# A four-layer graph network: more gathers in flight, source tables split from on-chip memory, and a new order of the steps in layer 1's edge stage

## The chip, the cores and the metric

One core of one Trainium2 chip runs the whole kernel. The time is the device time of one execution in microseconds. Matrix products run on TensorE (PE), element-wise work on VectorE (DVE) and ScalarE (ACT), indirect DMAs are issued by GpSimd (POOL), most plain DMAs by SyncE (SP).

## What is computed

Node features x (6250 nodes, 64 wide) go through four graph layers; each ends in a residual addition and a layer norm. There are 206250 edges (src, dst), sorted by dst, with 64 features each. Layer 0 is a hypergraph convolution, layer 1 an edge network, layer 2 a gated convolution, layer 3 a LightGCN sum. The change touches layers 1 and 2:

```python
# layer 1, H = 128
edge_in = concatenate([edges, nodes[receivers], nodes[senders]])
h = relu(edge_in @ We1 + be1)
agg = segment_sum(h @ We2 + be2, receivers)
# layer 2
gate = sigmoid(k[dst] + q[src])
agg = segment_sum(gate * v[src], dst)
```

For layer 1 the two node products are made once per node: one table for target rows (tab[4]) and one for source rows (tab_src[4]), both 128 wide. An edge then adds its target row, its source row and its own features times a 64x128 weight, takes the relu and is summed at its target node.

## The kernel before, in words

**Windows and chunks.** The nodes stand in NB = 49 blocks of 128. Each block of target nodes has a window of 36 tiles of 128 edges. In layer 1, 25 of the windows (the slots kind) hold their edges sorted by source block into 49 groups of 128 slots, so that the source rows as well as the target rows can be picked by PE with 0/1 selection matrices. The other 24 (the natural kind) keep their edges in their own order; there only the target row is picked by PE, and the source rows are fetched from tab_src in HBM by POOL, with one indirect DMA (gather) per tile of 128 edges. A slots window is worked off in 7 chunks of 7 blocks, a natural one in 6 chunks of 6 tiles. One window of each kind makes a pair: 13 steps, alternating slots, natural, ..., slots, numbered q = 0 to 12. There are 24 pairs, and a last slots window with 7 steps. Twenty-four natural windows of 36 tiles make 864 gathers.

**Tables in three parts.** For exact products every f32 table is split into three bf16 parts: ACT copies to bf16 (first part), DVE subtracts (rest), ACT copies again (second part), DVE subtracts (third part); L1693, L2251, L1697 and L2255, in seven pieces each. Before a layer's edge stage two tables are split: the target table (dtab into dsplit) and the source table (qtab into qsplit). Both are first stored from the arena (NW, NV) to HBM (L767 to L771) and loaded again by SP (L645, L647), because the target table needs another node order. NW and NV hold the linear layer's results; NV is copied out of PSUM by ACT. Layer 2 uses the same routine with a target table 64 wide. In layer 1 POOL gathers need the stored source table; in layer 2 nothing does but the load.

**The order of a step in layer 1's edge stage (edge_pairs, one function on each engine).** Each engine has its own queue, in program order, and waits on semaphores. In step q, before the change:
- SP (load_pair, L676 to L691) loads the selection rows and features of the chunk; rings of four slots and three natural buffers.
- PE (body, L1386): transposes the features of chunk q (transpose_features, L1325), makes the pre-activation of chunk q-2 by selecting rows and multiplying features (meet: L1348 source rows, L1353 target rows, L1359 features), and sums the messages of chunk q-4 at their targets (add_up, L1379).
- ACT (body, L1757): copies the transposed features out of PSUM (keep_features, L1734; two fT buffers, so that it waits for PE's meet of q-2), stores the selection matrices of slots chunks for layer 2 (store_hots), and takes the relu of chunk q-2 (messages: L1744 slots, L1747 natural). A natural relu waits for DVE's addition of the gathered rows, a slots relu for PE's meet and for the sum of the chunk before last, whose hid buffer it takes.
- DVE (body, L2421): for a natural chunk adds the gathered rows to the pre-activation of q-2 (add_sources, L2381), makes the row selection of q (L2347), then the residual (second part) of the messages of q-2 (L2394), the sum selection of q (L2330 slots, L2364 natural) and the last part of q-2 (L2401). PE's add_up waits for the last part.
- POOL (gather_sources, L943) issues the gathers (L967) into a ring of three qgot buffers. Before each it waits until the one four tiles earlier has landed (LIVE = 4 semaphores feat_put), and before a chunk that reuses a buffer for DVE's addition. At the start of each pair it loads the pair's source row numbers (gidx, L953) and waits for them.

Before this, POOL's queue holds the feature puts (put_features, L920), 900 indirect DMAs that place the edge features into the slots layout; they began in the stage before layer 0.

```python
def earlier(j, odd, q, back):
    return (j, odd, q - back) if q >= back else (j - 1, 1 - odd, SEQ + q - back)
...
    act.wait_ge(fT_made, count_at(j, q))
    if not isinstance(j, int) or j > 0 or q >= 2:
        act.wait_ge(pre_made, count_at(j, q) - 2)
```

Of the kernel before, what the change touches and what calls it, by code (L numbers as in the profile page):

```python
# [19 lines left out]
E = 206250  # L20
D = 64
H = 128
# [43 lines left out]
def build(nc, x, src, dst, feat, W1, b1, W2, b2, We1, be1, We2, be2, Wn1, bn1, Wn2, bn2,  # L66
# [11 lines left out]
    with ctx:  # L78
# [46 lines left out]
        NV = carve(76, NB * H).rearrange("p (b f) -> p b f", b=NB)  # L125
# [126 lines left out]
        dtab = carve(73.5, NB * H)  # L252
        qtab = carve(98, NB * H)
# [118 lines left out]
        tabs_in = [sem(f"tabs_in{i}") for i in range(2)]  # L372
# [35 lines left out]
        gate_out = sem("gate_out")  # L408

# [26 lines left out]
        TAB_STORES = [16, 32, 48, 64, 32, 64, 80]  # L436
# [103 lines left out]
        def gathers_landed(eng, j, tiles):  # L540

            for i in range(LIVE):
                if tiles > i:
                    eng.wait_ge(feat_put[i], j * (PUTS * 16) + (NS * PUTS * 16 + (tiles - i + LIVE - 1) // LIVE * 16))

        @block.sync
        def _(sp):
# [93 lines left out]
            def slots(k):  # L641
# [4 lines left out]
                    .then_inc(tabs_in[0], 16)  # L646
                sp.dma_start(qtab, nodes(tab_src[k])).then_inc(tabs_in[1], 16)  # L647
# [87 lines left out]
            def general(k):  # L735
                w = W_TAB[k]
                sp.wait_ge(tab_stored_g if k < 4 else tab_stored, TAB_STORES[k])

# [24 lines left out]
            for k in range(4, 7):  # L763
                w = W_TAB[k]
                sp.wait_ge(tab_ready, k + 1)
                if k == 4:
                    sp.dma_start(nodes(tab[4]), NW[:, :, :].rearrange("p b f -> p (b f)")).then_inc(tab_stored, 16)  # L767
                    sp.dma_start(nodes(tab_src[4]), NV[:, :, :].rearrange("p b f -> p (b f)")).then_inc(tab_stored, 16)
                elif k == 5:
                    sp.dma_start(tab[5].rearrange("(p b) f -> p b f", p=P), NW[:, :, 0:D]).then_inc(tab_stored, 16)  # L770
                    sp.dma_start(nodes(tab_src[5]), NV[:, :, :].rearrange("p b f -> p (b f)")).then_inc(tab_stored, 16)  # L771
                else:
                    sp.dma_start(tab[k].rearrange("(p b) f -> p b f", p=P), NW[:, :, 0:D]).then_inc(tab_stored, 16)
# [16 lines left out]
        def _(pool):  # L790
# [21 lines left out]
            def general(k):  # L812
                w = W_TAB[k]
                pool.wait_ge(tab_stored_g if k < 4 else tab_stored, TAB_STORES[k])
                idx = lambda c: bass.IndirectOffsetOnAxis(ap=gcol[:, c:c + 1].bitcast(u32), axis=0)
# [127 lines left out]
            def gather_sources():  # L943

                pool.wait_ge(tab_stored, TAB_STORES[4])
                pool.wait_ge(splits_lo, 2 * NC)

                def body(j, odd, first=False):
                    start = pool.value_load(start_i[0:1, bass.ds(j + NS, 1)], min_val=0, max_val=E - WE)
                    if not isinstance(j, int) or j >= 2:  # L950
                        for i in range(LIVE):
                            pool.wait_ge(feat_put[i], j * (PUTS * 16) + (NS - 1) * (PUTS * 16))
                    pool.dma_start(gidx[odd][:, :], src[bass.ds(start, WE)].rearrange("(p t) -> p t", p=P)).then_inc(gidx_in, 16)  # L953
                    for n in range(NCH):
# [7 lines left out]
                        for t in range(TN):  # L962
                            tile = n * TN + t
                            i = tile % LIVE
                            pool.wait_ge(feat_put[i], j * (PUTS * 16) + (NS * PUTS * 16 + tile // LIVE * 16))
                            pool.nop(nofuse=True)
                            pool.indirect_dma_start(qgot[n % 3][:, slot_of[t] * P:(slot_of[t] + 1) * P], None, tab_src[4],  # L967
                                                    bass.IndirectOffsetOnAxis(ap=gidx[odd][:, tile:tile + 1].bitcast(u32), axis=0))\
                                .then_inc(feat_put[i], 16)
                body(0, 0, first=True)  # L970
                body(1, 1)
                with pool.Fori(1, PAIRS_N // 2) as i:
                    body(i * 2, 0)
                    body(i * 2 + 1, 1)

# [11 lines left out]
        def _(pe):  # L987
# [321 lines left out]
            def edge_pairs():  # L1309
# [182 lines left out]
        def _(act):  # L1492
# [190 lines left out]
            def slots(k):  # L1683
# [42 lines left out]
            def edge_pairs():  # L1726
# [9 lines left out]
                def messages(j, odd, q):  # L1736

                    kind, c = place(j, q)
                    i = (q + odd) % 2
                    if kind == "slots":  # L1740
# [64 lines left out]
        def _(dve):  # L1805
# [434 lines left out]
            def slots(k):  # L2240
# [4 lines left out]
                for i, (tb, sp_, wd) in enumerate(((dtab, dsplit, w_), (qtab, qsplit, H))):  # L2245
                    t3 = tb[:, 0:NB * wd].rearrange("p (b f) -> p b f", b=NB)
                    s3 = sp_[:, 0:NB * 3 * wd].rearrange("p (b s f) -> p b s f", b=NB, s=3)
                    with dve.Fori(0, NC) as c:
                        at = bass.ds(c * CH, CH)
                        dve.wait_ge(splits_hi, c + (1 + NC * (2 * m + i)))  # L2250
                        V.tensor_tensor(t3[:, at, :], t3[:, at, :], s3[:, at, 0, :], ALU.subtract).then_inc(splits_res, 1)  # L2251
# [300 lines left out]
```

## Time and profile before

| | us |
|---|---|
| median of 3 runs | 4964.16 (4954.04 to 4967.15) |
| the profiled execution, its own time | 4958.28 |
| its span | 4956.7 |
| busy in the span: PE / PE weight load | 4118.4 (83%) / 3710.4 (75%) |
| busy: DVE / ACT / POOL | 3063.9 (62%) / 1450.4 (29%) / 2552.3 (51%) |
| mean granted TensorE clock | 0.92 |

The busy shares are means over stages with different limits, so a change in one stage is read from that stage's windows, waits and timelines. Idle time in brackets stands before the instruction it belongs to, with what ended it. x3 means three instructions merged into one row, with the time from the first one's start to the last one's end. Matmuls are pipelined, and the end that a row shows overlaps the next one's start by up to 0.16 us, so that steps are measured from start to start.

### The profile page before, as it was taken

The page shows a single profiled execution, that of the slowest core. Times are in us where ns is not written, and L with a number is a line of the kernel's source. Part 1 is how long each engine was busy: PE and PEld are TensorE (multiplying, and loading weights), DVE is VectorE, ACT ScalarE, POOL GpSimd, SP SyncE. Part 2 cuts the span into 40 slices and gives each one's busy share as a digit, 9 for nine tenths or more (in the row PEclk, how much of TensorE's full clock was granted, in tenths as well). Part 3 has the DMA queues.
Part 4 walks back from the last instruction along what each step waited for, and adds up shares of the span by engine and source line. Part 5 has one row for each costly group of instructions (what it writes and reads, how often), then busy time and mean ns, then how long its engine had stood idle before and what let it go on. Part 6 is the DMA issues. An engine that isn't in the chain of part 4 may idle for free.

```text
span 4956.7 us, 144137 instructions
## 1 busy us (share of the span) xinstructions
PE 4118.4 (83%) x56332; PEld 3710.4 (75%) x56332; DVE 3063.9 (62%) x4215; ACT 1450.4 (29%) x2353; POOL 2552.3 (51%) x2291
## 2 busy tenths in 40 slices
PE   1777799987999981999999999899758989999596
PEld 0566688887999981777777777777548988888596
DVE  5999888881111023777777777777437777777612
ACT  0333599990000012222222222222222222222100
POOL 0388766665665676666666666666003433333200
PEclk9766899998999995999999999999859999999798
DMA  5510488889999955776676777677326766666496
GB/s 173 203 30 29 144 317 321 323 320 315 397 383 417 417 199 187 226 232 220 227 235 228 227 235 229 224 230 236 128 78 219 235 207 205 221 221 214 135 399 260
DMA packets 430602, 1170.77 MB, mean 236 GB/s; under 512 B 111223, under 2 KB 250470, under 8 KB 422760
## 3 DMA queue, kind: packets, MB, share of 16 engines
q1 hardware_dynamic: 331910, 929.09, 53.0%
q0 software_dynamic: 66016, 114.12, 7.9%
q10 hardware_dynamic: 32256, 121.34, 6.2%
q8 instruction: 340, 5.57, 0.4%
q14 instruction: 80, 0.66, 0.0%
HBM read 798.21 MB, written 368.14 MB: 235 GB/s over the span
## 4 chain that ended last, share of the span: by engine, by line
DMA 41%; issue 27%; POOL 16%; PE 9%; DVE 4%; POOLq 2%; SPq 1%; ACT 0%; ACTq 0%; DVEq 0%
DMA feat_slot<-SK,sidx_p 18%; DMA arena<-tab_l_src,SK 17%; POOL arena L843 6%; POOL feat_slot L920 5%; POOL arena L967 4%; PE PS L1254 4%; DMA sidx_p<-SK 2%; DMA SK<-in_src_dram 2%; PE PS L1422 1%; PE PS L1023 1%; PE PS L1426 0%; SPq L460 0%; POOLq L890 0%; SPq L461 0%; PE PS L1442 0%
## 5 line engine op out<-in xcount | busy, mean ns | idle before, releaser
L920 POOL DMA_INDIRECT feat_slot<-SK,sidx_p x900 | 1114.1, 1238 | 568.7 <-DMA feat_slot<-SK,sidx_p 294.7
L967 POOL DMA_INDIRECT arena<-tab_l_src,SK x864 | 976.5, 1130 | 525.0 <-DMA arena<-tab_l_src,SK 241.8
L843 POOL TENSOR_TENSOR arena<-arena 128x448 f32<-128x448 f32 x343 | 365.6, 1066 | 808.6 <-DVE arena L2287 808.6
L1422 PE MATMUL PS<-arena 128*128 128x128 bf16 x7203 | 651.8, 221 | 124.5 <-DVE arena L2330 64.9
L1254 PE MATMUL PS<-arena 128*128 128x192 bf16 (+1 forms) x7203 | 615.4, 248 | 107.5 <-DVE arena L2130 61.9
L1254 PEld LDWEIGHTS PS<-arena 128*128 128x128 bf16 x7203 | 607.0, 98 | 114.4 <-DVE arena L2130 62.2
L1426 PE MATMUL PS<-arena 128*128 (+1 forms) x7203 | 610.4, 194 | 0.0
L1353 PE MATMUL PS<-arena 128*128 (+1 forms) x6267 | 591.4, 223 | 0.0
L1422 PEld LDWEIGHTS PS<-arena 128*128 128x128 bf16 x7203 | 457.4, 99 | 148.0 <-issue 138.0
L1426 PEld LDWEIGHTS PS<-arena 128*128 128x128 bf16 x7203 | 446.0, 99 | 1.1
L1353 PEld LDWEIGHTS PS<-arena 128*128 128x128 bf16 x6267 | 427.8, 100 | 3.8
L1379 PE MATMUL PS<-arena 128*128 128x384 bf16 x2089 | 414.9, 336 | 2.1 <-DVE arena L2401 2.1
L1348 PE MATMUL PS<-arena 128*128 128x128 bf16 x3675 | 408.1, 220 | 7.5 <-DVE arena L2330 7.5
L2394 DVE TENSOR_TENSOR arena<-arena 128x896 f32<-128x896 f32 (+1 forms) x319 | 328.4, 1029 | 125.0 <-ACT arena L1744 112.3
L1711 ACT ACTIVATE arena<-PS 128x448 f32<-128x448 f32 x343 | 186.8, 544 | 730.1 <-PE PS L1426 730.1
L1190 PE MATMUL PS<-arena 128*128 128x128 bf16 x4802 | 344.9, 220 | 39.8 <-DVE arena L2076 19.5
L1325 PE MATMUL PS<-ident,arena 128*128 128x128 f32 x1132 | 184.5, 281 | 228.4 <-ACT arena L1734 124.2
L2280 DVE TENSOR_TENSOR arena<-arena,PS 128x448 f32<-128x448 f32 x343 | 212.0, 618 | 240.1 <-ACT arena L1711 217.6
L2076 DVE TENSOR_TENSOR arena<-sd,iota 128x1792 bf16<-128x1792 bf16 x343 | 351.7, 1083 | 10.1 <-DMA nat_rows<-arena 10.1
L2381 DVE TENSOR_TENSOR arena<-PS,arena 128x768 f32<-128x768 f32 x144 | 137.8, 957 | 351.6 <-DMA arena<-tab_l_src,SK 308.4
L1325 PEld LDWEIGHTS PS<-ident,arena 128*128 128x128 f32 x1132 | 137.7, 142 | 289.3 <-issue 133.2
L1359 PE MATMUL PS<-wtwo,arena 64*128 64x128 f32 x4178 | 349.4, 294 | 0.0
(254 smaller groups left out, 6957.0 us busy)
## 6 DMA issues: line engine op xcount, KB each, us to landing
arena<-slot_rows SPq DMA_DIRECT2D x343, 448.0 KB
arena<-cnt_t SPq DMA_DIRECT2D x147, 896.0 KB
hots<-arena ACTq DMA_DIRECT2D x175, 672.0 KB
arena<-hots SPq DMA_DIRECT2D x175, 672.0 KB
arena<-cnt_t SPq DMA_DIRECT2D x147, 672.0 KB
cnt_t<-arena SPq DMA_DIRECT2D x49, 1568.0 KB
cnt_s<-arena SPq DMA_DIRECT2D x49, 1568.0 KB
arena<-cnt_s SPq DMA_DIRECT2D x49, 896.0 KB
```

Of the source, the lines that this page charges most:

```text
L843: pool.tensor_tensor(hid3[i][:, 2 * n:3 * n], hid3[i][:, n:2 * n], upper3[i][:, n:2 * n], ALU.subtract)\
L920: pool.indirect_dma_start(feat_slot, bass.IndirectOffsetOnAxis(ap=sidx_p[odd][:, n:n + 1].bitcast(u32), axis=0), fwin[h][:, t * D:(t + 1) ...
L967: pool.indirect_dma_start(qgot[n % 3][:, slot_of[t] * P:(slot_of[t] + 1) * P], None, tab_src[4], bass.IndirectOffsetOnAxis(ap=gidx[odd][:, ...
L1190: last = nc.tensor.matmul(to[:, cut], one[:, cut], two[:, cut], start=True, stop=True)
L1254: last = nc.tensor.matmul(PS[:, at:at + w3], ring[u % RING][:, of:of + P], esplit[:, (i * CH + w) * w3:(i * CH + w + 1) * w3], start=u == ...
L1348: nc.tensor.matmul(PS[:, to:to + P], selp[c % 4][:, cut], qsplit[:, (of * 3 + s) * H:(of * 3 + s + 1) * H], start=s == 0 and b < 2, stop=F ...
L1353: nc.tensor.matmul(PS[:, to:to + P], (selp[c % 4] if kind == "slots" else seln[c % 3])[:, cut], table, start=kind == "natural" and s == 0 ...
L1359: last = nc.tensor.matmul(PS[:, to:to + P], fT[i][rows, n * P:(n + 1) * P], wtwo[rows, :], start=False, stop=True, skip_group_check=True)
L1379: last = nc.tensor.matmul(o, hot[:, b * P:(b + 1) * P], parts[:, :, order[b], :], start=c == 0 and b == 0, stop=c == end and b == n - 1)
L1422: last = nc.tensor.matmul(PS[:, to:to + P], selS[c][:, cut], qsplit[:, (b * 3 + s) * H:(b * 3 + s + 1) * H], start=s == 0, stop=False, ski ...
L1426: last = nc.tensor.matmul(PS[:, to:to + w_], selT[c][:, cut], dsplit[:, bass.ds(of + s * w_, w_)], start=False, stop=s == 2, skip_group_ch ...
L2076: V.tensor_tensor(hot_c[c].rearrange("p (b s a) -> p b s a", b=PAIR, a=4), sd4[odd][:, c * PAIR * 4:(c + 1) * PAIR * 4].rearrange("p (b s ...
```

## The change

- POOL keeps six gathers in flight instead of four: tile t of a chunk waits on a semaphore of its own (q_in[t]) for the same tile of the chunk before. The source row numbers of a pair are loaded during the pair before, after its second chunk's gathers, and those of the first pair ahead of the waits for the tables.
- Before layers 1 and 2 the source table is no longer loaded back. It is split first, straight from NV, with the rest in a buffer of its own (qrest); the target table follows. In layer 1 the source table is stored after the target table's load has been issued, and POOL waits for that store (src_stored). In layer 2 it isn't stored at all on this path. NV, dtab and the rest move within the arena.
- In layer 1, PE's step begins with add_up of q-4; transpose of q and meet of q-2 follow.
- ACT takes the relu of a natural chunk in the step after (q-3), behind keep_features of q. The relu of a slots chunk stays at q-2.
- DVE makes residual and last part of a natural chunk in the step after (q-3), behind add_sources of q-2 and ahead of the row selection of q. For slots chunks nothing changes.

The diff, cut to its core:

```diff
@@ -249,8 +249,8 @@
 
         qsplit = carve(0, NB * 3 * H, bf16)
         dsplit = carve(36.75, NB * 3 * H, bf16)
-        dtab = carve(73.5, NB * H)
-        qtab = carve(98, NB * H)
+        qrest = carve(100, NB * H)
+        dtab = carve(124.5, NB * H)
         hots_c = [carve(73.5 + 5.25 * c, HOTS, bf16) for c in range(NC)]
         sel_c = [hot[:, 0:PAIR * P] for hot in hots_c]
         selS = [sel[:, 0:CH * P] for sel in sel_c]
...
@@ -643,8 +639,10 @@
                 w_ = W_TAB[k]
                 sp.wait_ge(tab_stored, TAB_STORES[k])
                 sp.dma_start(dtab[:, 0:NB * w_].rearrange("p (b f) -> p b f", b=NB), tab[k].rearrange("(b p) f -> p b f", p=P))\
-                    .then_inc(tabs_in[0], 16)
-                sp.dma_start(qtab, nodes(tab_src[k])).then_inc(tabs_in[1], 16)
+                    .then_inc(dtab_in, 16)
+                if k == 4:
+                    sp.dma_start(nodes(tab_src[4]), NV[:, :, :].rearrange("p b f -> p (b f)")).then_inc(src_stored, 16)
+                    sp.wait_ge(src_stored, 16)
                 sp.wait_ge(splits_lo, 2 * NC * (m + 1))
 
                 def load(j, kept, between=True):
...
@@ -942,15 +942,11 @@
 
             def gather_sources():
 
-                pool.wait_ge(tab_stored, TAB_STORES[4])
-                pool.wait_ge(splits_lo, 2 * NC)
-
-                def body(j, odd, first=False):
+                def fetch_sources(j, odd):
                     start = pool.value_load(start_i[0:1, bass.ds(j + NS, 1)], min_val=0, max_val=E - WE)
-                    if not isinstance(j, int) or j >= 2:
-                        for i in range(LIVE):
-                            pool.wait_ge(feat_put[i], j * (PUTS * 16) + (NS - 1) * (PUTS * 16))
                     pool.dma_start(gidx[odd][:, :], src[bass.ds(start, WE)].rearrange("(p t) -> p t", p=P)).then_inc(gidx_in, 16)
+
+                def body(j, odd, first=False, more=True):
                     for n in range(NCH):
                         if n >= 3:
                             pool.wait_ge(q_added, j * NCH + (n - 2))
@@ -961,17 +957,25 @@
                         pool.nop(nofuse=True)
                         for t in range(TN):
                             tile = n * TN + t
-                            i = tile % LIVE
-                            pool.wait_ge(feat_put[i], j * (PUTS * 16) + (NS * PUTS * 16 + tile // LIVE * 16))
-                            pool.nop(nofuse=True)
+                            if not first or n > 0:
+                                pool.wait_ge(q_in[t], j * (NCH * 16) + n * 16)
+                                pool.nop(nofuse=True)
                             pool.indirect_dma_start(qgot[n % 3][:, slot_of[t] * P:(slot_of[t] + 1) * P], None, tab_src[4],
                                                     bass.IndirectOffsetOnAxis(ap=gidx[odd][:, tile:tile + 1].bitcast(u32), axis=0))\
-                                .then_inc(feat_put[i], 16)
+                                .then_inc(q_in[t], 16)
+                        if n == 1 and more:
+                            fetch_sources(j + 1, 1 - odd)
+
+                fetch_sources(0, 0)
+                pool.wait_ge(src_stored, 16)
+                pool.wait_ge(splits_lo, 2 * NC)
                 body(0, 0, first=True)
                 body(1, 1)
-                with pool.Fori(1, PAIRS_N // 2) as i:
+                with pool.Fori(1, PAIRS_N // 2 - 1) as i:
                     body(i * 2, 0)
                     body(i * 2 + 1, 1)
+                body(PAIRS_N - 2, 0)
+                body(PAIRS_N - 1, 1, more=False)
 
             for k in range(7):
                 if k == 4:
...
@@ -1385,10 +1389,11 @@
 
                 def body(j, odd, first=False):
                     for q in range(NC if isinstance(j, int) and j == PAIRS_N else SEQ):
+                        if q >= 4 or not first:
+                            add_up(*earlier(j, odd, q, 4))
                         transpose_features(j, odd, q)
-                        for lag, part in ((2, meet), (4, add_up)):
-                            if q >= lag or not first:
-                                part(*earlier(j, odd, q, lag))
+                        if q >= 2 or not first:
+                            meet(*earlier(j, odd, q, 2))
                 pairs(pe, body)
                 for q in range(NC - 2, NC):
                     meet(PAIRS_N, 0, q)
...
@@ -1685,16 +1690,19 @@
                 w_ = W_TAB[k]
                 turns = TURNS[k]
                 hid_, upper_ = (hid, upper) if k == 4 else (hid3, upper3)
-                for i, (tb, sp_, wd) in enumerate(((dtab, dsplit, w_), (qtab, qsplit, H))):
-                    act.wait_ge(tabs_in[i], 16 * (m + 1))
+                act.wait_ge(lin_kept_q, UNITS["l1pq"] * (m + 1))
+                for i, (tb, sp_, wd, rest) in enumerate(((NV.rearrange("p b f -> p (b f)"), qsplit, H, qrest), (dtab, dsplit, w_, dtab))):
+                    if i == 1:
+                        act.wait_ge(dtab_in, 16 * (m + 1))
                     t3 = tb[:, 0:NB * wd].rearrange("p (b f) -> p b f", b=NB)
+                    r3 = rest[:, 0:NB * wd].rearrange("p (b f) -> p b f", b=NB)
                     s3 = sp_[:, 0:NB * 3 * wd].rearrange("p (b s f) -> p b s f", b=NB, s=3)
                     with act.Fori(0, NC) as c:
                         nc.scalar.activation(s3[:, bass.ds(c * CH, CH), 0, :], t3[:, bass.ds(c * CH, CH), :], ACT.Copy)\
                             .then_inc(splits_hi, 1)
                     with act.Fori(0, NC) as c:
                         act.wait_ge(splits_res, c + (1 + NC * (2 * m + i)))
-                        nc.scalar.activation(s3[:, bass.ds(c * CH, CH), 1, :], t3[:, bass.ds(c * CH, CH), :], ACT.Copy)\
+                        nc.scalar.activation(s3[:, bass.ds(c * CH, CH), 1, :], r3[:, bass.ds(c * CH, CH), :], ACT.Copy)\
                             .then_inc(splits_mid, 1)
 
                 if k == 4:
...
@@ -1757,13 +1767,15 @@
                 def body(j, odd, first=False):
                     for q in range(NC if isinstance(j, int) and j == PAIRS_N else SEQ):
                         keep_features(j, odd, q)
+                        if q >= 3 or not first:
+                            messages(*earlier(j, odd, q, 3), "natural")
                         if q >= 2 or not first:
                             store_hots(*earlier(j, odd, q, 2))
-                            messages(*earlier(j, odd, q, 2))
+                            messages(*earlier(j, odd, q, 2), "slots")
                 pairs(act, body)
                 for q in range(NC - 2, NC):
                     store_hots(PAIRS_N, 0, q)
-                    messages(PAIRS_N, 0, q)
+                    messages(PAIRS_N, 0, q, "slots")
                 for i in range(4):
                     act.wait_ge(hots_put[i], NS * (16 if i == 3 else 32))
 
...
@@ -2376,7 +2389,8 @@
                     dve.wait_ge(pre_made, count_at(j, q))
                     if not isinstance(j, int) or j > 0 or q >= 2:
                         dve.wait_ge(agg_made, count_at(j, q) - 2)
-                    gathers_landed(dve, j, (c + 1) * TN)
+                    for t in range(TN):
+                        dve.wait_ge(q_in[t], j * (NCH * 16) + (c + 1) * 16)
                     n = TN * H // 2
                     V.tensor_tensor(hid[i][:, 0:TN * H].rearrange("p (k n) -> p k n", k=2),
                                     PS[:, i * 1024:(i + 1) * 1024].rearrange("p (k n) -> p k n", k=2)[:, :, 0:n],
...
@@ -2421,15 +2435,17 @@
                 def body(j, odd, first=False):
                     for q in range(NC if isinstance(j, int) and j == PAIRS_N else SEQ):
                         old = None if first and q < 2 else earlier(j, odd, q, 2)
+                        older = None if first and q < 3 else earlier(j, odd, q, 3)
                         if old:
                             add_sources(*old)
+                        if older and place(older[0], older[2])[0] == "natural":
+                            residual(*older)
+                            last_part(*older)
                         select_rows(j, q)
                         if old and place(old[0], old[2])[0] == "slots":
                             residual(*old)
                         select_sums(j, q)
-                        if old and place(old[0], old[2])[0] == "natural":
-                            residual(*old)
-                        if old:
+                        if old and place(old[0], old[2])[0] == "slots":
                             last_part(*old)
                         if q == 3 and not first:
                             keep_natural(j - 1)
```

## Rows read from the trace of the kernel before

**Rows 1.** Stage table: us, busy of PE, PEld, DVE, ACT, POOL; PEclk, DMA.

```profile
200.00:500.00 300.00, 222.61 (x2979) 183.28 (x2979) 296.81 (x297) 110.92 (x340) 257.67 (x159) 0.71 0.10 29
1975.20:3545.60 1570.40, 1430.96 (x17174) 1174.76 (x17174) 1118.41 (x1507) 438.96 (x633) 983.28 (x880) 0.97 0.69 226
```

**Rows 2.** List of waits, 2230 to 3400 us: waited for, total us, times, longest.

```profile
DVE arena L2381 <- DMA arena<-tab_l_src,SK: 216.7, 79, 7.6
...
PE PS L1325 <- ACT arena L1734: 73.6, 46, 4.4
```

**Rows 3.** Groups, POOL, 2230 to 3400 us: busy, mean ns, idle before.

```profile
L967 POOL DMA_INDIRECT arena<-tab_l_src,SK x661 | 746.4, 1129 | 411.9 <-DMA arena<-tab_l_src,SK 192.9 <-issue 152.3 <-DMA SK<-in_src_dram 60.8
L953 POOL DMA_DIRECT2D SK<-in_src_dram x18 | 10.6, 591 | 2.2 <-DMA arena<-tab_l_src,SK 2.0
```

**Rows 4.** Timeline, PE, a cycle without waits: start us, us, what, count.

```profile
2607.95 0.60 PE L1325 MATMUL PS<-ident,arena 128*128 128x128 f32 x4
...
2611.92 1.37 PE L1379 MATMUL PS<-arena 128*128 128x384 bf16 x7
2613.12 0.49 PE L1325 MATMUL PS<-ident,arena 128*128 128x128 f32 x3
2613.45 1.17 PE L1353 MATMUL PS<-arena 128*128 x18
...
2616.45 0.60 PE L1325 MATMUL PS<-ident,arena 128*128 128x128 f32 x4
```

**Rows 5.** Timeline, POOL and DVE: layer 1's first gather and first addition.

```profile
1963.21 0.59 POOL L953 DMA_DIRECT2D SK<-in_src_dram  x1
1966.23 1.00 POOL L967 DMA_INDIRECT arena<-tab_l_src,SK  x1 [2.42 <-DMA SK<-in_src_dram]
...
1975.18 0.96 DVE L2381 TENSOR_TENSOR arena<-PS,arena 128x768 f32<-128x768 f32 x1 [31.11 <-DMA arena<-tab_l_src,SK]
```

**Rows 6.** Timeline, ACT and DVE: the splits before layer 2.

```profile
3705.21 3.39 ACT L1693 ACTIVATE arena<-arena  x7 [27.26 <-DMA arena<-tab]
...
3710.46 4.54 DVE L2255 TENSOR_TENSOR arena<-arena  x7
...
3721.97 7.09 DVE L2255 TENSOR_TENSOR arena<-arena  x7
```

**Rows 7.** Chain that ended last: store and load of layer 3's table.

```profile
4696.68 9.04 DMA tab<-arena
4705.78 10.04 DMA arena<-tab
```

**Rows 8.** Timeline, ACT, layer 1: fT copies (L1734) and what follows.

```profile
2610.33 0.84 ACT L1747 ACTIVATE arena<-arena 128x768 f32<-128x768 f32 x1 [2.92 <-DVE arena L2381]
2612.08 0.60 ACT L1734 ACTIVATE arena<-PS 128x512 f32<-128x512 f32 x1 [0.91 <-PE PS L1359]
...
2621.63 0.58 ACT L1734 ACTIVATE arena<-PS 128x512 f32<-128x512 f32 x1
2622.11 0.91 ACT L1744 ACTIVATE arena<-PS 128x896 f32<-128x896 f32 x1
```

**Rows 9.** Timeline, DVE, layer 1: a natural chunk, then a slots chunk.

```profile
2611.21 0.96 DVE L2394 TENSOR_TENSOR arena<-arena 128x768 f32<-128x768 f32 x1
2612.20 0.96 DVE L2401 TENSOR_TENSOR arena<-arena 128x768 f32<-128x768 f32 x1
...
2613.54 0.88 DVE L2347 TENSOR_SCALAR arena<-arena,pnum 128x1792 bf16<-128x1792 bf16 x1
...
2615.88 1.08 DVE L2401 TENSOR_TENSOR arena<-arena 128x896 f32<-128x896 f32 x1
```

**Rows 10.** Timeline, DVE and PE: the stage's last part and last sum.

```profile
3543.02 1.09 DVE L2401 TENSOR_TENSOR arena<-arena 128x896 f32<-128x896 f32 x1
...
3544.17 1.36 PE L1379 MATMUL PS<-arena 128*128 128x384 bf16 x7 [2.13 <-DVE arena L2401]
```

**Rows 11.** Timeline, PE: three of the twelve waits over 2.3 us before L1325.

```profile
1999.27 0.84 PE L1325 MATMUL PS<-ident,arena 128*128 128x128 f32 x3 [2.34 <-ACT arena L1734]
1999.91 2.12 PE L1353 MATMUL PS<-arena 128*128 128x128 bf16 x18
...
3189.08 0.55 PE L1325 MATMUL PS<-ident,arena 128*128 128x128 f32 x3 [3.38 <-ACT arena L1734]
...
3357.22 0.65 PE L1325 MATMUL PS<-ident,arena 128*128 128x128 f32 x4 [2.44 <-issue]
```

More of the change, by code:

```diff
@@ L124, in build @@
         NW = carve(51, NB * H).rearrange("p (b f) -> p b f", b=NB)
-        NV = carve(76, NB * H).rearrange("p (b f) -> p b f", b=NB)
+        NV = carve(75.5, NB * H).rearrange("p (b f) -> p b f", b=NB)
         TB = carve(101, NB * (D + 1))
@@ L371, in build @@
         splits_lo = sem("splits_lo")
-        tabs_in = [sem(f"tabs_in{i}") for i in range(2)]
+        dtab_in = sem("dtab_in")
+        src_stored = sem("src_stored")
         slot_in = [sem(f"slot_in{c}") for c in range(NC)]
@@ L408, in build @@
         gate_out = sem("gate_out")
+        q_in = added[4:7] + [gate_in, gate_out, ft_in]
         block = ctx.enter_context(nc.Block())
@@ L435, in build @@
         SOURCES = [1, 3, 6]
-        TAB_STORES = [16, 32, 48, 64, 32, 64, 80]
+        TAB_STORES = [16, 32, 48, 64, 16, 32, 48]
         ON_V = (2, 5)
@@ L737, in general @@
                 sp.wait_ge(tab_stored_g if k < 4 else tab_stored, TAB_STORES[k])
+                if k in (4, 5):
+                    sp.dma_start(nodes(tab_src[k]), NV[:, :, :].rearrange("p b f -> p (b f)")).then_inc(src_stored, 16)
                 z = acc[k].rearrange("(r p) f -> p r f", p=P)
@@ L814, in general @@
                 pool.wait_ge(tab_stored_g if k < 4 else tab_stored, TAB_STORES[k])
+                if k in (4, 5):
+                    pool.wait_ge(src_stored, 16 * (k - 3))
                 idx = lambda c: bass.IndirectOffsetOnAxis(ap=gcol[:, c:c + 1].bitcast(u32), axis=0)
@@ L943, in gather_sources @@
             def gather_sources():
-                pool.wait_ge(tab_stored, TAB_STORES[4])
-                pool.wait_ge(splits_lo, 2 * NC)
-                def body(j, odd, first=False):
+                def fetch_sources(j, odd):
                     start = pool.value_load(start_i[0:1, bass.ds(j + NS, 1)], min_val=0, max_val=E - WE)
-                    if not isinstance(j, int) or j >= 2:
-                        for i in range(LIVE):
-                            pool.wait_ge(feat_put[i], j * (PUTS * 16) + (NS - 1) * (PUTS * 16))
                     pool.dma_start(gidx[odd][:, :], src[bass.ds(start, WE)].rearrange("(p t) -> p t", p=P)).then_inc(gidx_in, 16)
+                def body(j, odd, first=False, more=True):
                     for n in range(NCH):
@@ L1734, in keep_features, with messages @@
                     nc.scalar.activation(fT[(q + odd) % 2][:, 0:n], PS[:, 2048:2048 + n], ACT.Copy).then_inc(fT_kept, 1)
-                def messages(j, odd, q):
+                def messages(j, odd, q, only):
                     kind, c = place(j, q)
                     i = (q + odd) % 2
+                    if kind != only:
+                        return
                     if kind == "slots":
@@ L2244, in slots @@
                 hid_, upper_ = (hid, upper) if k == 4 else (hid3, upper3)
-                for i, (tb, sp_, wd) in enumerate(((dtab, dsplit, w_), (qtab, qsplit, H))):
+                for i, (tb, sp_, wd, rest) in enumerate(((NV.rearrange("p b f -> p (b f)"), qsplit, H, qrest), (dtab, dsplit, w_, dtab))):
                     t3 = tb[:, 0:NB * wd].rearrange("p (b f) -> p b f", b=NB)
+                    r3 = rest[:, 0:NB * wd].rearrange("p (b f) -> p b f", b=NB)
                     s3 = sp_[:, 0:NB * 3 * wd].rearrange("p (b s f) -> p b s f", b=NB, s=3)
@@ L2250, in slots @@
                         dve.wait_ge(splits_hi, c + (1 + NC * (2 * m + i)))
-                        V.tensor_tensor(t3[:, at, :], t3[:, at, :], s3[:, at, 0, :], ALU.subtract).then_inc(splits_res, 1)
+                        V.tensor_tensor(r3[:, at, :], t3[:, at, :], s3[:, at, 0, :], ALU.subtract).then_inc(splits_res, 1)
                     with dve.Fori(0, NC) as c:
@@ L2254, in slots @@
                         dve.wait_ge(splits_mid, c + (1 + NC * (2 * m + i)))
-                        V.tensor_tensor(s3[:, at, 2, :], t3[:, at, :], s3[:, at, 1, :], ALU.subtract).then_inc(splits_lo, 1)
+                        V.tensor_tensor(s3[:, at, 2, :], r3[:, at, :], s3[:, at, 1, :], ALU.subtract).then_inc(splits_lo, 1)
                 if k == 4:
```

5 lines of the change are left out of this document (removed).

## The prediction, made before the changed kernel was seen to run

> **What bounds the kernel now.** I read the stage table first, then the waits, POOL's groups, and the timelines of one cycle. Layer 1's edge stage holds 1570 of the 4957 us, from the first addition of gathered rows to the last sum [rows 1]. PE is busy for 1431 of them and looks like the bound. The waits say otherwise: in 1170 us, DVE's addition L2381 waits 217 us for gathers, and PE's transposes 74 us for ACT [rows 2]. POOL's gathers take 746 us and the idle time before them 412, together nearly all of the stretch: 193 went to earlier gathers, 61 to row numbers, 152 to issue [rows 3]. Waiting for DVE does not show among them, so POOL is never ahead.
>
> What does PE need? Where nothing waits, the slots step takes 2613.12 - 2607.95 = 5.17 us and the natural step 2616.45 - 2613.12 = 3.33 [rows 4]. A pair of windows has seven and six: 56.2 us; the last window's seven steps take 36, and five steps (22 us) are done before the stage begins. So 24 x 56.2 + 14 = 1363 would do, and a pair now takes (1570 - 14) / 24 = 64.8. The 8.6 us between are waits that stem from gathers: late gather, late addition, ACT's relu stuck, the fT copy behind it, PE's transposes.
>
> **The change, part by part.** The sum goes against the profiled execution (4958.3 us; span 4956.7), which is 5.9 below the median of 4964.2.
>
> *Six gathers in flight, row numbers early.* POOL keeps 36 gathers of 1.13 us [rows 3] with 0.3 before each (the 152 us of issue over 661 are 0.23, and some issue time hides in the other waits, so a little more): 51.5 us a pair, and 0.6 for the moved load of row numbers. The load is issued behind 12 gathers, and nobody needs it until 24 more are out. What waits is 193 + 61 us of 1170, 14 us a pair, and most of it goes. POOL then needs 52 to 53 us and follows the others. Alone this would give up to the 8.6 us a pair, if nothing else held PE.
>
> *Source table split from SBUF.* In layer 1 the first gather came at 1966.2, after feature puts and a wait for the row numbers alone [rows 5]: POOL's queue, not the splits, sets it. Splits done earlier just wait there: gain 0, between -10 and +10 since DVE's splits now lie beside other puts. The store of the source rows, now behind the other table's load, has the same cover; without the puts it would cost about what layer 2 gains. There, ACT's idle 27.3 us before 3705.21 began at 3678.0, with the tables ready, and the last split ended at 3721.97 + 7.09 = 3729.1 [rows 6]. Now the source split runs at once and takes 2 x 7.1 on DVE, until about 3693. The target table makes a store and a load, which took 9.0 + 10.0 us for layer 3's table of the same size [rows 7]; it lands at 3697.1. Its split took from 3705.2 to 3715.0, 9.8 us: done at 3706.9. Gain 22 us. PE, SP and POOL follow the splits there.
>
> *PE sums four steps back first; relu, residual and last part of natural chunks come a step later.* This decides. Let q be a slots step. PE now does: sum q-4, transpose q, select q-2. On ACT the relu of natural chunk q-3 has moved behind the fT copy of q. That copy waits until PE has selected q-2, because it reuses its fT buffer: the last work of PE's step. And PE's next step begins with the sum of chunk q-3. So this chain runs while PE stands still:
> - the fT copy starts 0.16 us after PE has left its selection (2611.92 [rows 4] to 2612.08), and what follows it on ACT 0.48 later (2621.63 to 2622.11) [rows 8];
> - relu to residual 0.88 (2610.33 [rows 8] to 2611.21), residual to last part 0.99, last part 0.96 [rows 9];
> - last part to PE's sum 0.06: DVE's 1.09 us one began at 3543.02, PE at 3544.17 [rows 10].
>
> Together 3.5 us. Before, relu, residual and last part of that chunk ran while PE selected the next one, and its sum stood at the end of that step; that cover is gone. After the wait PE has a natural step, 3.33 us. In that time DVE does the slots chunk: last part 0.88, then row selection to last part, 2613.54 to 2616.96, 3.4 us [rows 9], 5.3 from the residual on. PE reaches the slots sum at 1.95 + 0.06 + 3.33 = 5.3: no further wait, no slack. The cycle is 5.17 + 3.33 + 3.5 = 12.0 us instead of 8.5. The trace of before has no such wait. Its bounds are 2.9 (the chain without the copy) and 4.4 (PE's longest wait for ACT [rows 2]); I take 3.5, the sum of its links. Six in a pair make 21 us.
>
> *The clock.* Twelve times in this stage PE waited over 2.3 us before L1325; the first, one more and the last are shown [rows 11]. After the first one the 18 matmuls of L1353 ran 2.12 us; they run 1.17 at full speed [rows 4]. Eight of the twelve steps came out 1.3 to 1.9 us longer, at the lower level, 1.2 GHz; four by 0.2 or less (3189.08 is one, after 3.38 idle). The mean is 1.05 a wait. PE's whole cycle is now on the path, so it adds in full: 6.3 us a pair, with bounds 0 and 6 x 1.9.
> The Trainium skill ("TensorE: Matmul & The Clock Gate", section "HAM oscillation — how this bites in real kernels") says that long enough waits between bursts make every burst start at half clock; this speaks against the change. By it each wait would cost what the eight cost, about 1.5, 65 us more in all than my sum. Four of the twelve rows disagree with "every".
>
> **The sum.** 56.2 + 21 + 6.3 = 83.5 us a pair, 24 x 83.5 + 14 = 2018 us for the stage, +448. Less 22 in layer 2: +426. That is 5384 on the profiled execution, 5390 on the median.
>
> **Rivals.**
> *A, faster: PE runs through.* The wait before the natural sum is covered after all, and the gathers pay: the stage takes 1363, -207, and -22: 4735. For it: POOL is the limit today [rows 3]. Against it: the order of the queues, in which the relu can come no earlier. Its place is ACT's natural relu, and it decides if the wait is under ((1570 + 22 - 14) / 24 - 56.2) / 6 = 1.6 us a natural chunk. 12%.
> *B: gathers stay the limit.* Six in flight land no faster together, and PE's new wait falls into time lost anyway: only layer 2's 22 go, 4942. For it: the DMA engines are busy 0.69 of the stage [rows 1]. Against: it needs A's condition too. 3%.
> The Trainium skill ("Trainium Kernel Development and Optimization", section "Key Constraints") says that the queues of SP, ACT and POOL all share 16 DMA engines, which would be B's cause; no row here separates it from latency.
> *C: the clock stays down.* From 200 to 500 us PE is busy 223 of 300 us, in short pieces, and the granted clock is 0.71 [rows 1]. The new cycle idles 3.5 of 12, about as much. At 0.71, PE's 56.2 become 79: 24 x (79 + 21) + 14 / 0.71 = 2420, +850 - 22, so 5792. Against: after the twelve waits speed was back within a step. 9%.
>
> **How the numbers follow.** My case has 76%, at 5390. Clock costs of 0 to 1.5 and a wait of 3.2 to 3.8 give it 5200 to 5500. The range, 5190 to 5560, goes a little further towards C and leaves out A, B and most of C. Faster by over 0.3%, about what a measurement of this kernel can tell: A and most of B, 0.14. Within 0.3%: 0.02. Slower: my case and C, 0.84.
>
> **What would show it.** Right: PE idle some 3.5 us before L1379 for natural chunks, released by DVE's last part, over 140 times, 450 to 520 us in all; ACT's natural relu held up by the copy and so by PE, not by DVE; POOL waiting for DVE's addition and hardly for gathers; DVE's addition not waiting for gathers; a stage clock near 0.93; layer 2's splits over 29 us after the tables, not 51; the first gather still near 1966. Wrong: a stage under 1570 us in which PE does not wait (A), DVE still waiting for gathers (B), a clock near 0.7 (C).

## The result, and the profile after

The changed kernel takes 5499.96 us in the median of three executions (5482.75 to 5503.73), against 4964.16: 1.109 of before, 95% interval 1.106 to 1.112. The profiled execution took 5499.96, its span is 5498.4 and the mean granted clock 0.888.

Layer 1's edge stage, the columns as in [rows 1]:

```profile
1957.90:4114.20 2156.30, 1627.18 (x17174) 1365.93 (x17174) 1107.11 (x1507) 421.19 (x632) 896.96 (x880) 0.87 0.51 164
```

It grew from 1570 to 2156 us with the same instructions, and its clock fell from 0.97 to 0.87. It begins 17.3 us earlier than before; what comes after it takes 1384.2 us instead of 1411.1. +585.9 - 17.3 - 26.9 is the 541.7 by which the span grew. Where [rows 2] had DVE waiting for gathers, the waits of the changed kernel from 2230 to 3400 us are these:

```profile
ACT arena L1742 <- PE PS L1363: 938.8, 171, 8.0
POOL arena L963 <- DVE arena L2395: 549.5, 79, 11.7
...
PE PS L1383 <- DVE arena L2415: 286.0, 92, 3.6
...
DVE arena L2395 <- DMA arena<-tab_l_src,SK: 22.0, 9, 2.5
```

L1383 is PE's sum, L2415 DVE's last part, L1742 the fT copy, L1363 PE's last matmuls of a selection, L2395 the addition. POOL now waits for DVE, and its group answers to [rows 3]:

```profile
L963 POOL DMA_INDIRECT arena<-tab_l_src,SK x477 | 488.7, 1025 | 680.0 <-DVE arena L2395 549.5 <-issue 130.5
```

In this stretch no gather waits for a gather any more, and none for row numbers. PE waits instead, in every cycle at the same place. PE's timeline over one cycle, which took 8.5 us in [rows 4]:

```profile
2604.95 1.21 PE L1383 MATMUL PS<-arena 128*128 128x384 bf16 x6 [3.46 <-DVE arena L2415]
2605.98 0.82 PE L1329 MATMUL PS<-ident,arena 128*128 128x128 f32 x3
2606.60 2.13 PE L1357 MATMUL PS<-arena 128*128 x18
2608.65 1.28 PE L1363 MATMUL PS<-wtwo,arena 64*128 64x128 f32 x12
2609.87 1.36 PE L1383 MATMUL PS<-arena 128*128 128x384 bf16 x7
2611.07 0.60 PE L1329 MATMUL PS<-ident,arena 128*128 128x128 f32 x4
...
2613.94 1.16 PE L1363 MATMUL PS<-wtwo,arena 64*128 64x128 f32 x14
2618.57 1.19 PE L1383 MATMUL PS<-arena 128*128 128x384 bf16 x6 [3.47 <-DVE arena L2415]
```

ACT and then DVE in the same wait:

```profile
2615.20 0.60 ACT L1742 ACTIVATE arena<-PS 128x512 f32<-128x512 f32 x1 [4.67 <-PE PS L1363]
...
2615.69 0.83 ACT L1757 ACTIVATE arena<-arena 128x768 f32<-128x768 f32 x1
2616.43 0.91 ACT L1754 ACTIVATE arena<-PS 128x896 f32<-128x896 f32 x1
```

```profile
2610.34 0.96 DVE L2395 TENSOR_TENSOR arena<-PS,arena 128x768 f32<-128x768 f32 x1 [2.31 <-PE PS L1363]
...
2616.56 0.96 DVE L2408 TENSOR_TENSOR arena<-arena 128x768 f32<-128x768 f32 x1 [4.47 <-ACT arena L1757]
2617.55 0.96 DVE L2415 TENSOR_TENSOR arena<-arena 128x768 f32<-128x768 f32 x1
2618.43 0.68 DVE L2360 TENSOR_SCALAR arena<-arena,pnum 128x1792 bf16<-128x1792 bf16 x1
```

PE's selection ends at 2615.10; the fT copy follows at 2615.20, the relu (L1757) at 2615.69, the residual at 2616.56, the last part at 2617.55, PE's sum at 2618.57. ACT had nothing to do for 4.67 us before the copy. DVE's addition for this relu ended at 2611.30, so the relu could have run from then on, but it stands behind the copy in ACT's queue. The cycle takes 2618.57 - 2604.95 = 13.6 us.

### The profile page after: what moved, and what is told of

Read it like the earlier page. It is cut to its first block, busy times and chain, and to the rows that moved or that the text cites. A ratio compares the mean times of both kernels' runs of the same rounds, so it can differ in the third digit from the quotient of the medians.

```text
span 5498.4 us, 144047 instructions
## 1 busy us (share of the span) xinstructions
PE 4314.7 (78%) x56332; PEld 3900.5 (71%) x56332; DVE 3053.2 (56%) x4215; ACT 1433.3 (26%) x2353; POOL 2460.3 (45%) x2291
## 4 chain that ended last, share of the span: by engine, by line
PE 35%; DMA 20%; issue 19%; POOL 10%; DVE 9%; ACT 3%; ACTq 1%; POOLq 1%; SPq 1%; DVEq 0%
DMA feat_slot<-SK,sidx_p 16%; PE PS L1357 8%; PE PS L1383 7%; PE PS L1363 6%; POOL arena L843 6%; POOL feat_slot L920 4%; PE PS L1352 4%; PE PS L1258 4%; DVE arena L2415 3%; PE PS L1329 3%; DVE arena L2408 3%; ACT arena L1757 2%; DMA sidx_p<-SK 2%; ACTq L1765 1%; PE PS L1427 1%
## 5 line engine op out<-in xcount | busy, mean ns | idle before, releaser
L963 POOL DMA_INDIRECT arena<-tab_l_src,SK x864 | 890.1, 1030 | 1175.8 <-DVE arena L2395 927.2
L1383 PE MATMUL PS<-arena 128*128 128x384 bf16 x2089 | 436.7, 348 | 558.2 <-DVE arena L2415 558.2
L1427 PE MATMUL PS<-arena 128*128 128x128 bf16 x7203 | 651.2, 221 | 98.3 <-DVE arena L2343 60.3
L1357 PE MATMUL PS<-arena 128*128 (+1 forms) x6267 | 704.6, 255 | 0.0
L1383 PEld LDWEIGHTS PS<-arena 128*128 128x128 bf16 x2089 | 180.9, 99 | 725.7 <-DVE arena L2415 478.9
L1258 PEld LDWEIGHTS PS<-arena 128*128 128x128 bf16 x7203 | 606.3, 98 | 112.0 <-DVE arena L2142 62.0
L1742 ACT ACTIVATE arena<-PS 128x512 f32<-128x512 f32 (+1 forms) x319 | 175.3, 549 | 1749.4 <-PE PS L1363 1738.0
L1431 PE MATMUL PS<-arena 128*128 (+1 forms) x7203 | 610.4, 194 | 0.0
L1357 PEld LDWEIGHTS PS<-arena 128*128 128x128 bf16 x6267 | 537.9, 118 | 7.8
L1427 PEld LDWEIGHTS PS<-arena 128*128 128x128 bf16 x7203 | 456.9, 99 | 121.9 <-issue 111.8
L1431 PEld LDWEIGHTS PS<-arena 128*128 128x128 bf16 x7203 | 445.6, 99 | 1.3
L1352 PE MATMUL PS<-arena 128*128 128x128 bf16 x3675 | 426.6, 227 | 0.0
L1194 PE MATMUL PS<-arena 128*128 128x128 bf16 x4802 | 344.8, 220 | 40.5 <-DVE arena L2088 20.4
L1363 PE MATMUL PS<-wtwo,arena 64*128 64x128 f32 x4178 | 376.4, 311 | 0.0
L1363 PEld LDWEIGHTS PS<-wtwo,arena 64*128 64x128 f32 x4178 | 315.3, 212 | 43.4 <-issue 21.6
L1194 PEld LDWEIGHTS PS<-arena 128*128 128x128 bf16 x4802 | 288.0, 98 | 80.9 <-DVE arena L2088 31.6
```

The lines of the kernel that those rows point to most:

```text
L1194: last = nc.tensor.matmul(to[:, cut], one[:, cut], two[:, cut], start=True, stop=True)
L1258: last = nc.tensor.matmul(PS[:, at:at + w3], ring[u % RING][:, of:of + P], esplit[:, (i * CH + w) * w3:(i * CH + w + 1) * w3], start=u == ...
L1352: nc.tensor.matmul(PS[:, to:to + P], selp[c % 4][:, cut], qsplit[:, (of * 3 + s) * H:(of * 3 + s + 1) * H], start=s == 0 and b < 2, stop=F ...
L1357: nc.tensor.matmul(PS[:, to:to + P], (selp[c % 4] if kind == "slots" else seln[c % 3])[:, cut], table, start=kind == "natural" and s == 0 ...
L1363: last = nc.tensor.matmul(PS[:, to:to + P], fT[i][rows, n * P:(n + 1) * P], wtwo[rows, :], start=False, stop=True, skip_group_check=True)
L1383: last = nc.tensor.matmul(o, hot[:, b * P:(b + 1) * P], parts[:, :, order[b], :], start=c == 0 and b == 0, stop=c == end and b == n - 1)
```

## Experiments

Each experiment is compared with the kernel before on its own chip, where that took 4946 us (the first four below), 4957 (the next four) and 4952 (the last), each a median of six or seven executions, the furthest of them 0.4% away. The new order alone, the filled wait and each half of the order ran once; for the others the median of four executions is given. "A pair" is the time between the first and the last of the 144 additions over the 23.8 pairs between them: 63.6 us before, 88.3 in the changed kernel.

**The old order with everything else of the change.** On PE, ACT and DVE these parts go back, for DVE and ACT in the same way as for PE:

```diff
-                        if q >= 4 or not first:
-                            add_up(*earlier(j, odd, q, 4))
                         transpose_features(j, odd, q)
-                        if q >= 2 or not first:
-                            meet(*earlier(j, odd, q, 2))
+                        for lag, part in ((2, meet), (4, add_up)):
+                            if q >= lag or not first:
+                                part(*earlier(j, odd, q, lag))
```

> The changed kernel with the order of PE, ACT and DVE in layer 1's edge stage as before (sum last on PE; relu, residual and last part of natural chunks two steps back); six gathers in flight, early row numbers and the direct split stay. Chain theory (relu behind the fT copy, sum at the head of PE's step): PE does not wait for DVE any more, and since gathers no longer pace the stage it runs at 56 to 58 us a pair, stage about 1370 to 1410 us, whole about 4740 to 4790. Rival, the gathers are the harm (six in flight or the moved load slow the DMAs or POOL): the stage stays above 2000 us and the whole near 5500. Rival, gathers were never the limit before: the stage is near 1570, the whole about 4920.

Measured: 4815 us against 4946 of before, 0.974 (0.970 to 0.978); a pair takes 59.7 us. The new order is the whole loss, and the rest of the change is a gain of 2.6%. It came out 25 us above the expected range. Its waits from 2230 to 3200 us:

```profile
POOL arena L963 <- DVE arena L2392: 146.3, 89, 6.1
...
PE PS L1329 <- DMA arena<-feat_slot: 22.8, 14, 3.9
PE PS L1329 <- issue: 16.7, 8, 2.8
DVE arena L2392 <- DMA arena<-tab_l_src,SK: 15.5, 15, 4.3
```

DVE waits 15.5 us for gathers, where it had waited 217 in a stretch a fifth longer. Of the 3.5 us a pair that PE still spends over 56.2, its waits for feature loads and the idle time called issue are 2.4 (39.5 us in 970). This version beats both kernels.

**The relu ahead of the copy.** One line of the changed kernel moves:

```diff
-                        keep_features(j, odd, q)
                         if q >= 3 or not first:
                             messages(*earlier(j, odd, q, 3), "natural")
+                        keep_features(j, odd, q)
```

> The changed kernel with one edit: on ACT the relu of the natural chunk three steps back stands ahead of the fT copy instead of behind it. Chain theory: the relu then waits only for DVE's addition, which is done a step earlier, so the 3.5 us wait of PE before each natural sum goes; what is left is DVE's and the slots chain, 57 to 62 us a pair, whole 4750 to 4880. Rival, the wait comes from DVE's order (residual and last part of the natural chunk ahead of the row selection) or from PE's sum at the head of the step, whatever ACT does: PE still waits 2 us or more before each natural sum, the whole stays above 5200.

Measured: 4907 us, 0.991 of before (0.988 to 0.995); 64.1 us a pair. So 24 of the 88 us are the place of one ACT instruction. What is left are waits of about 1 us before the slots sum. PE's timeline:

```profile
2609.33 0.94 PE L1363 MATMUL PS<-wtwo,arena 64*128 64x128 f32 x12
2611.30 1.36 PE L1383 MATMUL PS<-arena 128*128 128x384 bf16 x7 [1.04 <-DVE arena L2415]
...
2616.47 1.19 PE L1383 MATMUL PS<-arena 128*128 128x384 bf16 x6
```

The natural sum at 2616.47 follows without a wait; the slots sum waits 1.04 us for DVE's last part, whose chunk had its relu behind the fT copy too. The range given reached 62 a pair and 4880, and both were passed by a little.

**The new order alone**, in the kernel before: the edits of PE, ACT and DVE as in the change, gathers and tables untouched.

> The kernel before with the new order of PE, ACT and DVE alone; four gathers in flight, late row numbers, both tables loaded back. Chain theory: the order costs by itself what the changed kernel costs, the slow gathers are hidden behind it: stage 2120 to 2180 us, whole 5500 to 5550 (layer 2's 22 us and the later start of layer 1 on top of the changed kernel). Rival, order and gathers harm only together: the whole below 5300.

Measured: 5519 us (1.116 of before) and 88.4 us a pair, like the changed kernel's 88.3. The late row numbers and four gathers in flight cost nothing under this order: the harm does not need the gathers' part, and hides its gain completely.

**PE's wait filled.** In the changed kernel PE issues work that nobody reads ahead of each natural sum:

```diff
+                    if kind == "natural":
+                        for _ in range(56):
+                            nc.tensor.matmul(PS[:, 2944:3072], identb[:, :], identb[:, :], start=False, stop=True, skip_group_check=True)
                     pe.wait_ge(msg_lo, count_at(j, q))
```

> The changed kernel with 56 extra matmuls of 128 columns into an unused part of the natural sum's PSUM bank, issued by PE where it waits before each natural sum (about 3.1 us at 2.4 GHz, inside the wait of 3.46). Clock theory (each wait drops the clock to 1.2 GHz for the work after it, 1.6 us a cycle): the granted clock in the stage rises from 0.87 to 0.98 or more, the cycle falls from 13.6 to about 12.0 us, the stage from 2156 to about 1920, the whole to about 5260. Rival, the extra 1.6 us is something else (operands, PSUM, DVE beside it): the cycle stays at 13.6 us or grows, the whole stays at 5500 or more.

Measured: 5319 us (1.075 of before), with 8064 more matmuls than the kernel that takes 5500 (1.109). PE's timeline in it (L1380 are the added ones):

```profile
2611.04 1.19 PE L1386 MATMUL PS<-arena 128*128 128x384 bf16 x6 [0.24 <-DVE arena L2418]
2612.07 0.49 PE L1329 MATMUL PS<-ident,arena 128*128 128x128 f32 x3
2612.40 1.17 PE L1357 MATMUL PS<-arena 128*128 x18
...
2619.54 3.30 PE L1380 MATMUL PS<-identb 128*128 128x128 bf16 x56
2623.07 1.20 PE L1386 MATMUL PS<-arena 128*128 128x384 bf16 x6 [0.23 <-DVE arena L2418]
```

The 18 matmuls take 1.17 us instead of 2.13, the cycle is 2623.07 - 2611.04 = 12.03 us, as the links gave without a clock cost, and the granted clock from 2300 to 2900 us is 0.98. So the 1.6 us a cycle are the clock. From the first addition to the last it is 170 us faster than the changed kernel (1929.6 against 2099.4), and as a whole 181 us, on another chip. 240 were expected; most of the rest is a stall that the changed kernel doesn't have there:

```profile
2572.46 1.22 PE L1380 MATMUL PS<-identb 128*128 128x128 bf16 x19 [2.11 <-issue]
2576.89 4.13 PE L1380 MATMUL PS<-identb 128*128 128x128 bf16 x37 [3.21 <-issue]
```

It comes once in each turn of the loop (two pairs, 163 us: the one before is at 2408.98), where PE waits for nothing that the profile shows, 5.3 us each, 53 us in the stage. Its cause is open.

**Each half of the order by itself**, the rest as in the changed kernel. First PE's sum at the head of the step, with ACT and DVE as before:

> The changed kernel with ACT's and DVE's order as before (relu, residual and last part of natural chunks two steps back) and PE's sum still at the head of its step. Chain theory: the relu comes right behind the addition again, so the natural sum is ready in time; only the slots sum stands closer behind DVE's last part, about 1 us of waiting a cycle: 61 to 65 us a pair instead of 88.3, first to last addition 1450 to 1545 us, whole 4830 to 4950. Rival, the sum's new place is the harm by itself: above 75 us a pair, whole above 5200.

Measured: 4916 us, 64.1 us a pair. Then the relu, residual and last part late, with PE's sum at the end of the step:

> The changed kernel with PE's sum at the end of its step as before, while ACT's relu and DVE's residual and last part of natural chunks stay a step later and behind the fT copy. Chain theory: the same 3.5 us chain runs while PE transposes and selects the next chunk (2.3 us) and sums the slots chunk before it (1.2), so it is nearly hidden: 60 to 64 us a pair, first to last addition 1430 to 1520 us, whole 4820 to 4940. Rival, the late relu is the harm by itself: above 75 us a pair, whole above 5200.

Measured: 4901 us, 62.7 us a pair. Against 59.7 with neither, one half costs 4.4 us a pair, the other 3.0, and both together 28.6. In the second, the chain runs while PE transposes, selects and sums another chunk. DVE's addition and selections come out late instead, and PE waits for the sum selection (L2342), here in us from 2230 to 3200:

```profile
PE PS L1352 <- DVE arena L2342: 47.3, 70, 0.7
```

**The halves of the gathers' part**, both with the old order and the direct split. Four in flight with early row numbers:

```diff
-                            if not first or n > 0:
-                                pool.wait_ge(q_in[t], j * (NCH * 16) + n * 16)
+                            if t >= 4:
+                                pool.wait_ge(q_in[t - 4], j * (NCH * 16) + (n + 1) * 16)
+                                pool.nop(nofuse=True)
+                            elif not first or n > 0:
+                                pool.wait_ge(q_in[t + 2], j * (NCH * 16) + n * 16)
```

> As e1_old_order (old order, early row numbers, direct split), but each gather waits for the one four back. If four in flight are what paced POOL, it waits for gathers again, some 190 us in 1170, and a pair takes 62 to 64 us instead of 59.7: whole 4860 to 4910. If the late row numbers alone were the limit, it stays at 59.7 a pair and 4815.

Measured: 4839 us, 0.977 (0.973 to 0.981), 60.2 us a pair. POOL does wait for gathers again, 151.7 us in 970, but late gathers rarely reach PE. Six in flight with row numbers loaded and awaited at the pair's start (fetch_sources(j, odd) at the head of POOL's body):

> As e1_old_order (old order, six in flight, direct split), but the row numbers of a pair are loaded at its start and waited for there. POOL has 53 us of work a pair and the load adds about 3.5, still under 59.7: if six in flight do it, the whole stays within 15 us of 4815; if the early load is what matters, a pair gains 3.5 us of waiting and the whole is at 4890 or more.

Measured: 4825 us, 0.972 (0.967 to 0.976), 59.8 us a pair; POOL waits 48.6 us in 970 for row numbers. Six in flight do it, as expected of that case. Neither expectation for four in flight held: it waits as the first had it, and yet costs only 0.5 us a pair, and its ratio can't be told from the 0.974 of both halves. So either half brings nearly the whole gain. From the traces, each alone takes POOL below PE's pace.

**The gathers' part alone** in the kernel before, without the direct split.

> The kernel before with the gathers' part alone: six in flight and early row numbers; old order, both tables loaded back. If the parts add up as read from the traces (e1_old_order is 0.9736 of before; layer 2's splits 22 us and the start of layer 1 some 12 to 17 us are the direct split's), this is about 95 us below before: ratio 0.981, with 59.7 us a pair, layer 2's splits again over 51 us after the tables. Rival, the start of layer 1 has nothing to do with the split: the first addition comes at 1958 to 1963 us here too, ratio 0.978 or less.

Measured: 4860 us, 0.981 (0.978 to 0.984), 59.6 us a pair, the last of layer 2's splits 51 us after the tables, the first addition at 1972.4 and not at 1958 to 1963. So most of the earlier start of layer 1 comes from the direct split.

## Why the prediction was right, and where its sums were off

The forecast was 5390 us, the range 5190 to 5560, and 5500 was measured: the mechanism was right, the sum too small. 5500 is the upper end of what the prediction gave its own case; the range reached further only towards C. The stage took 138 us more than forecast, and an earlier start and a shorter rest gave back 22. The deciding step, that the relu behind the fT copy and the sum at the head of PE's step leave PE idle for a chain through ACT and DVE, is shown: moving the relu takes the wait away, the new order alone makes it, and its length was the sum of its links.

Against the 1363 us in which PE would run through, the stage has 793 us more; the prediction had 655.
- *The chain*: after the first natural sum of the stage PE waits before each of the other 143, 3.46 us in the mean, 495 us. Predicted 144 of 3.5, 504.
- *The clock*: this term was mis-sized. It had 1.05 us a wait, 151 us, as the mean of "twelve" waits. The trace of before has 22 waits over 2.3 us before L1325 behind the stage's first; with the missing ten the mean is 1.3 a wait and the term about 190 us. The regular wait costs more than that: of the 141 steps behind a wait from 1990 to 4060 us, 139 are 1.5 to 2.4 us longer than at full speed, 237 us together, and two are not. The granted clock over the slowed step at 2604.95 is 0.65, over the slots step behind it and over the step at 2031.00 it is 1.00; the stage clock came out as 0.87 and not near 0.93. The first rows show a slowed step in the trace of before (18 matmuls in 2.13 us instead of 1.17), the second one of the two steps at full speed in the changed kernel (four transposes in 0.60 us; in the slowed step at 2118.65 they take 1.05):

```profile
2552.54 0.90 PE L1325 MATMUL PS<-ident,arena 128*128 128x128 f32 x3 [3.51 <-ACT arena L1734]
2553.24 2.13 PE L1353 MATMUL PS<-arena 128*128 x18
```

```profile
2031.00 1.19 PE L1383 MATMUL PS<-arena 128*128 128x384 bf16 x6 [3.36 <-DVE arena L2415]
2032.03 0.60 PE L1329 MATMUL PS<-ident,arena 128*128 128x128 f32 x4
```

By the Trainium skill ("TensorE: Matmul & The Clock Gate", section "HAM oscillation — how this bites in real kernels"), long enough waits start every burst at half clock. Here 139 of 141 did, and with the prediction's 65 us for that rule the term would have been 216. Filling the wait shows that it is the clock.

- *The change of windows*: the prediction repeated one cycle. At a pair's end two slots chunks follow each other, and the slots sum waits about 1 us more, 24 us in the stage. Waits for feature loads in the last window are 6 us, the part of the first wait that lies in the stage 4. Some 20 us are left and were not taken apart.

*Source table*: in layer 2 the tables were ready at 4247 and the last split ended at 4276.1, 29 us later, as worked out: 22 us gained. DVE's rows:

```profile
4248.51 7.10 DVE L2264 TENSOR_TENSOR arena<-arena  x7 [1.32 <-ACT arena L1701]
4255.53 7.09 DVE L2268 TENSOR_TENSOR arena<-arena  x7
4267.16 4.37 DVE L2264 TENSOR_TENSOR arena<-arena  x7 [4.54 <-ACT arena L1701]
4271.52 4.54 DVE L2268 TENSOR_TENSOR arena<-arena  x7
```

The 4.54 us of waiting is for the target table, as predicted. In layer 1 the gain was put at 0, at most 10, and was 17 us in the changed kernel's trace (first addition 1957.9 instead of 1975.2), some 10 of it between the two kernels that differ in the split alone (1962.6 and 1972.4). The first gather came at 1949.0 and not near 1966. The step that failed is that POOL's queue sets the start whatever the tables do: POOL is the bound there, but its puts ran beside the table traffic. In the trace of before one put waited 6.5 us and the row numbers behind another 7.0 while tables were stored, loaded and split; after, no wait in that stretch exceeds 1.9. That this is the cause was only read from the traces.

*Gathers*: right that they bound the stage before and stop doing so (only "never ahead" went too far: in the 1170 us POOL waited three times for DVE, 5.9 us). Of the up to 8.6 us a pair that they could give, 3.9 came out under the old order (63.6 to 59.7); of the 3.5 that are left above 56.2, feature loads and issue are 2.4.

Of the rivals, A fell: the wait is 3.46 us, above its 1.6. Its condition was made true by the old order, and then the kernel is faster, as A said, though by 131 us and not 229. B fell: POOL's waits for gathers are gone. C fell: the clock is 0.87, not 0.71, and in the step after the slowed one PE is back at full speed.

## What to carry to other kernels

Moving a step later gives it slack only if everything that stands ahead of it in its queue is done earlier too: look at what the instruction is queued behind, not only at what it waits for. Two orders that cost 4.4 and 3.0 us a pair alone cost 28.6 together here, because one moves the producer later and the other the consumer earlier; so add up the chain between them across all queues before trying both. A repeated wait of PE can cost more than its own length: here 3.46 us, and 1.7 for the slow work behind it. When single waits are to give the price of that, take all of them in the stage.

## What the runs showed of the hardware that was not expected

- Of the 22 single waits of 2.3 to 6.6 us in the kernel before, 16 slowed the work behind them, four as short as 2.32 to 2.44 us among them, and one of 3.38 did not. The same wait of 3.46 us in every cycle slowed it in 139 of 141 cases. Work that nobody reads, put into that wait, took 170 us off the 2099 between first and last addition.
- A loop of PE that is 672 matmuls a turn longer stalls 5.3 us in each turn on nothing that the profile shows. Shorter ones exist in other kernels too (8 in 970 us in the version with the old order, up to 2.8 us each, 16.7 in all).
- One put of POOL takes 0.97 us, but 1.70 while DVE subtracts f32 tables (1901.70 to 1924 in the trace of before). In 970 us of gathers at six in flight, POOL waits 14.2 us for landing, at four in flight 151.7.
